# Raising TensorE's counts by a drain behind a group of matmuls, in a four-layer graph network

## The reference

```python
edge_index = jnp.stack([src, dst])
h = jnp.maximum(_layernorm(x, axis=-1), 0.0)
x = x + _L0_gnn_ref(h, edge_attr3_2x32, src, dst, ...)   # attention, softmax messages, summed by dst
...
x = x + _L1_gnn_ref(h, edge_index, 12500)                # segment_sum(h[src], dst)
...
x = x + _L2_gnn_ref(h, edge_index, edge_attr_4, edge_attr_8, 12500, ...)
# per edge: silu(silu(radial @ W1 + b1) @ W2 + b2) @ W3 + b3 gives 256 weights, multiplied with h[src] and summed by dst
...
x = x + _L3_gnn_ref(h, edge_index, ...)                  # 4-head attention, softmax over the edges of one src
```

## Time and profile before

| what | us |
|---|---|
| median of three runs without a profile | 9832.66 |
| lowest and highest of them | 9832.34, 9836.29 |
| span of the profiled execution | 12916.5 |
| busy in that span: TensorE matmuls | 5065.7 (39%) |
| weight loads | 2933.9 (23%) |
| VectorE | 6996.1 (54%) |
| ScalarE | 3814.9 (30%) |
| GpSimd | 7314.1 (57%) |

### The profile page before, as it was taken

One profiled execution on the slowest core, in us unless ns is written; L12 is line 12 of the kernel. 1 busy time (PEld: TensorE's weight loads), 2 busy tenths in 40 slices (PEclk: granted clock), 3 DMA queues, 4 the chain that ended last, 5 costly groups with the idle time before them and its releaser, 6 DMA issues. The chain is left out here.

```text
span 12916.5 us, 85174 instructions
## 1 busy us (share of the span) xinstructions
PE 5065.7 (39%) x24874; PEld 2933.9 (23%) x25115; DVE 6996.1 (54%) x11023; ACT 3814.9 (30%) x6015; POOL 7314.1 (57%) x7495
## 2 busy tenths in 40 slices
PE   2224300029135555555536777777613333300001
PEld 1214300002124444444422222222211111100001
DVE  5654488889452222222226777777614545457761
ACT  0002333336013333333312222222102333346640
POOL 5645577758554444444455556556563555566654
PEclk5556655569556666666667777777756666655555
DMA  6101366635300000000010111111010111133331
GB/s 237 45 20 39 112 219 212 213 128 184 110 20 15 17 17 17 17 15 17 16 31 21 24 22 23 23 23 25 21 19 1 44 32 31 35 93 126 122 101 39
DMA packets 466546, 815.90 MB, mean 63 GB/s; under 512 B 229189, under 2 KB 326902, under 8 KB 415526
## 3 DMA queue, kind: packets, MB, share of 16 engines
q10 hardware_dynamic: 81600, 447.60, 9.0%
q0 software_dynamic: 236352, 156.57, 6.9%
q1 hardware_dynamic: 148134, 206.27, 4.9%
HBM read 402.58 MB, written 407.23 MB: 63 GB/s over the span
## 5 line engine op out<-in xcount | busy, mean ns | idle before, releaser
L1609 POOL DMA_INDIRECT hs<-tab_h,src_i x3136 | 2975.3, 949 | 2771.9 <-issue 1164.6
L1201 POOL DMA_INDIRECT en<-tab_s,src_i x1568 | 1562.9, 997 | 863.9 <-issue 508.4
L1096 DVE SCALAR_TENSOR_TENSOR picked<-rank_ps,hot_hi 128x98 f32<-128x98 f32 x1568 | 313.1, 255 | 2131.9 <-remote 1139.7
L1888 PE MATMUL tp_ps<-w_pair,x 128*128 128x512 f32 x1568 | 1092.3, 786 | 569.8 <-DVE prod_b L2016 495.9
L2298 POOL DMA_INDIRECT rows_src<-out_rows,pos x784 | 750.7, 957 | 742.5 <-ACT out_rows L2344 468.0
L2420 DVE TENSOR_SCALAR hot_col<-count_up,pos_late 128x784 bf16<-128x784 f32 x560 | 564.9, 1029 | 747.2 <-remote 552.8
L2310 POOL DMA_INDIRECT hs<-tab_h,ptr x784 | 741.5, 946 | 378.2 <-issue 256.2
L2323 PE MATMUL late_ps<-hot_col,hot_row 128*128 128x512 bf16 x1075 | 517.8, 493 | 1010.0 <-DVE hot_col L2420 567.6
L997 PE MATMUL rank_ps<-place_sb,hot_t 128*128 128x98 f32 x3136 | 840.6, 385 | 0.0
L2013 DVE TENSOR_TENSOR prod_a<-tp_ps,zz 128x768 f32<-128x768 f32 x392 | 374.4, 955 | 721.4 <-remote 534.5
L1035 PE MATMUL turn_bank<-place_sb,ident 128*128 128x98 f32 x784 | 231.1, 389 | 1240.4 <-issue 634.9
(11 more groups left out here) (402 smaller groups left out, 16214.5 us busy)
## 6 DMA issues: line engine op xcount, KB each, us to landing
sums<-rows ACTq DMA_DIRECT2D x98, 1088.0 KB
sums<-rows ACTq DMA_DIRECT2D x147, 512.0 KB
ev_rows<-zeros ACTq DMA_DIRECT2D x16, 3136.0 KB
en_rows<-en SPq DMA_DIRECT2D x49, 1024.0 KB
raw<-ev_rows ACTq DMA_DIRECT2D x49, 1024.0 KB
en_back<-en_rows ACTq DMA_DIRECT2D x49, 1024.0 KB
r<-in_edge_attr_2x ACTq DMA_DIRECT2D x49, 1024.0 KB
y_rows<-r ACTq DMA_DIRECT2D x49, 1024.0 KB
```

Source lines behind the costliest of these rows:

```text
L1201: pool.indirect_dma_start(en[s][:, g, :], None, tab_s0, bass.IndirectOffsetOnAxis(ap=src_i[:, p * 2 * CH + g:p * 2 * CH + g + 1], axis=0)) ...
L1609: pool.indirect_dma_start(rows[k][:, g, :], None, tab_h, bass.IndirectOffsetOnAxis(ap=src_i[:, t * CH + g:t * CH + g + 1], axis=0)).then_i ...
L1888: nc.tensor.matmul(o, x2[k][:, a, b * EP:(b + 1) * EP], w3_cols, start=True, stop=False)
```

## The change

Where the increment of a semaphore hung on the last matmul or transpose of a group, that instruction now has none, and a drain is issued behind it on TensorE that carries the increment. This is done at ten places; the waits of the other engines and their values stay.

```diff
@@ def turn
                 for g in range(GR):
-                    last = nc.tensor.transpose(self.turn_ps[:, g, 0:EP], self.hot_lo[k][:, q * GR + g, :], identb[0:EP, 0:EP])
-                last.then_inc(self.turned, 1)
+                    nc.tensor.transpose(self.turn_ps[:, g, 0:EP], self.hot_lo[k][:, q * GR + g, :], identb[0:EP, 0:EP])
+                nc.tensor.drain().then_inc(self.turned, 1)
@@ def rank
-                last.then_inc(self.ranked, 1)
+                nc.tensor.drain().then_inc(self.ranked, 1)
@@ def group
-                last.then_inc(self.samed, 1)
+                nc.tensor.drain().then_inc(self.samed, 1)
...
-                last.then_inc(self.placed, 1)
+                nc.tensor.drain().then_inc(self.placed, 1)
@@ def count, in stages A and B
-                    last.then_inc(counted, 1)
+                    nc.tensor.drain().then_inc(counted, 1)
@@ def hidden1
-                    last.then_inc(hid, 1)
+                    nc.tensor.drain().then_inc(hid, 1)
@@ def hidden2
-                    nc.tensor.matmul(hid_ps[:, u % 3, 0:4 * EP], w2[:, :], x1[:, a, :], start=True, stop=True).then_inc(hid, 1)
+                    nc.tensor.matmul(hid_ps[:, u % 3, 0:4 * EP], w2[:, :], x1[:, a, :], start=True, stop=True)
+                    nc.tensor.drain().then_inc(hid, 1)
@@ def products
-                    last.then_inc(tpw, 1)
+                    nc.tensor.drain().then_inc(tpw, 1)
@@ def late
-                        last.then_inc(late_added, 1)
+                        nc.tensor.drain().then_inc(late_added, 1)
```

## The result

The changed kernel takes 10575.82 us (median of 4 runs, 10540.91 to 10601.76) against 9832.5 us of the kernel before, run beside it: a ratio of 1.0755, 95% interval 1.0742 to 1.0768. It is 743 us slower. The forecast was 9960, with a range up to 10210.

The account below looks back on a forecast made before the run. GpSimd's pace of indirect DMAs was taken to set nearly all of the four main stages. Drain costs of 92 + 20 + 10 + 5 = 127 us on 9833 gave 9960 us, range 9815 to 10210.

Parts of the forecast that it names:

- The budget: Four main stages: 6634 indirect DMAs at 1.25 us, 8292 us, plus 1535 us of other span make 9827 us.
- A, C and D: First-layer gathers and 14 ranked chunks; tensor weights; pointer columns, sends and last gathers: drains add 20, 10 and 5 us.
- in the profile alone: Whole trace: 3084 us of the 12916.5 us span taken as waiting that timed runs lack.
- The price of a stop: On TensorE's queue, a drain delays the next weight load by 0.34 us, or 0.41 at half clock.
- The sum at the upper level: Ranked chunk in the second-layer stage at full clock: 17.1 us plus 2.5 for drains, 19.6, under GpSimd's 20.0.
- From place step to transposes: Rank group on TensorE: sign expected in the changed trace, 2.6 us instead of 1.95.
- I take a quarter at half clock: Second-layer stage, 84 ranked chunks: a quarter at half clock gives 21.1 us a chunk after, 92 us in all.
- Half clock: Rival, chance 0.15: drains lower TensorE's activity so most chunks fall to 1.2 GHz; 462 us in second-layer stage, 10336 total.
- the half-clock chunk: Ranked chunk in the second-layer stage at half clock: 22.6 us without late counts, 25.5 with drains.
- "Turned" and "samed": Two rank-group drains: turned's push of the own and cross matmuls put at 0.07 us; samed's hidden behind ScalarE's copy.
- The late counts are real: Rival, chance 0.12: late matmul counts hold 265 us of the timed median; drains' counts may come in time, giving 9695.

Follow-up runs that it names:

- light_placed_ranked: Kernel before with 12 of 16 indirect DMAs left out in the second-layer gather stage and drains for placed and ranked alone: 11827.48 us, ratio 0.9164.
- light_filler4: Changed kernel with 12 of 16 second-layer indirect DMAs left out and four extra, overwritten 512-column matmuls in every rank group: 12578.46 us, ratio 0.9740.
- light_before_2: Kernel before, without drains, with 12 of 16 indirect DMAs left out in the second-layer gather stage: 11546.36 us, ratio 0.8972.
- ranks_only: Kernel before with drains for the four rank counts alone (turned, samed, placed, ranked; 1568 drains): 13652.29 us, ratio 1.0598.

## Why the prediction was wrong

**The budget was right, what it said of the profile wrong.** GpSimd's pace sets A, C and D in the quick condition, within 43 us each, as 1.25 us an operation said. But "in the profile alone" fell: whole timed comparisons run at the 12916 us of the trace of before. That trace was a run of another condition than its timed runs, and its waits and clocks were those of TensorE held up by late counts.

**The price of a stop was right in size.** 0.41 us at 1.2 GHz was forecast, 0.42 is measured. At 2.4 GHz 0.34 was forecast: in light_placed_ranked a group takes 4.39 us from place step to place step against 3.60, 0.39 for each of its two.

```profile
5001.17 0.43 PE L1035 MATMUL turn_bank<-place_sb,ident 128*128 128x98 f32 x2 [0.49 <-ACT hot_t L1054]
...
5005.56 0.43 PE L1035 MATMUL turn_bank<-place_sb,ident 128*128 128x98 f32 x2 [0.49 <-ACT hot_t L1054]
```

The sum at the upper level held too: 19.6 us a chunk with all drains was forecast, 19.95 is the chunk at clock 1.00 in the result's trace. From place step to transposes it is 2.75 us in light_filler4 (5010.46 to 5013.21), where 2.6 was forecast. The drains end some 0.02 us behind the modelled end of the last matmul (median in the changed kernel), where the earlier trace rows gave 0.05, and the Trainium skill's rule in "PSUM — Partial Sum Buffer", "Engine vs sequencer instructions", that a drain waits until the engine is idle, agrees: the load behind the drain starts 0.49 us after the last matmul's start, not with it.

**The step that failed: "I take a quarter at half clock".** In the changed kernel all ranked chunks but a few run at half clock. The share was taken as a property of the stage, the same before and after, when the change itself moves it: 0.83 without drains and 0.51 with them, with the lateness out of the way. For the kernel before the quarter was good: 18.5 us a chunk by it, 18.7 in light_before_2, where one group of four is slow. The rival "Half clock" had this mechanism and was given 0.15. The argument against it, that the trace of before had more stalls than a timed run, pointed the wrong way: its 0.66 came with stalls of 10 us between bursts at 1.00, and a stream with four short stops a group and no long ones has 0.51. What the clock stood at with few long waits said nothing about what it is with many short ones.

**And the half-clock chunk was too small.** 25.5 us was forecast "with drains at 0.41 and less hidden"; it is 29.05. The prediction let only 2.9 us of drains through, 25.5 - 22.6. (The 22.6 came from a chunk that the earlier trace rows show at full clock near its end; that it lies close to the 22.3 below is luck.) At 1.2 GHz TensorE's own stream is the loop (5.58 us a group without drains), so no stop is hidden beside another engine's work: all 16 count, 16 x 0.42 = 6.7. "Turned" and "samed", costed at 0.07 and 0, are as dear as the other two. By the prediction's own formula, all chunks at half clock and none hidden: (29.05 - 20.0) x 84 = 760, where it had 92, and 462 for the rival. Either half alone would have cost little. At 1.2 GHz without a drain a chunk would be at least 4 x 5.58 = 22.3 (an estimate; no run had it); with all drains and the clock left where it was, 18.8 + 4.0 = 22.8 (an estimate, the sum of the two pairs), and 19.95 with the clock at 1.00. Over GpSimd's 20.0 that is 2.3, 2.8 or nothing, at most some 240 us in 84 chunks. Together they make 760.

**A, C and D** were forecast at 20, 10 and 5 us. No more than 43, 35 and 35 can be there, what these stages stand over GpSimd's pace; how much is isn't shown. In the late condition the drains in C show, 223 us for 784 of them, 0.28 each where about 0.2 was put: C isn't at GpSimd's pace then.

**"The late counts are real" (0.12)** was nearly right in what it saw and wrong in what follows. The counts are late in timed runs, but only in the late condition, and a drain doesn't mend it: there the drains themselves end late. All records of the drain of `samed`, line 1029 (ns least, median, most; first and last start), first in ranks_only, then in the changed kernel of the result:

```profile
L1029 PEldq DRAIN  x392: 838/1570/10124, 1083.4 to 7289.4; - x196
```
```profile
L1029 PEldq DRAIN  x392: 927/1653/1655, 701.9 to 5534.6; - x196
```

## What to carry to other kernels

A drain in a stream of short matmul groups costs a stop, here 0.4 us, and the stops together can cost the clock, here 6 us of every 10: price both, and never carry the clock of the trace of before into the kernel after. Before a short stop is called hidden, do the sum at 1.2 GHz too, where TensorE may wait for nobody and so nothing hides. And if a trace's span doesn't match the timed runs, treat it as a trace of another condition: find a stage's floor from one engine's count and pace, and distrust its waits.

## What the runs showed of the hardware that was not expected

*More work made TensorE faster.* Two useless 512-column matmuls a group took a chunk from 29.05 to 24.5 us, clock 0.51 to 0.79. The Trainium skill's rule in "TensorE: Matmul & The Clock Gate", "Part 1: The HAM clock gate", that sustained activity lifts the throttle, has this direction.

*A stream busy for 2168 of 2691 us stayed at 1.2 GHz* for nearly the whole stage, and one busy for 1254 of 1837 had 0.83: the busy share of a row didn't tell the clock. (The same matmuls are busy for longer at 1.2 GHz.)

*Short stops kept the clock from coming back.* Without drains the clock came back within one group, 5.58 us, of an idle 3.71. With drains the same program ran a chunk in 19.95 us at 1.00 and then, behind an idle 2.11, at 0.50 for over 1100 us.

*Two conditions.* The kernel before took 9832 us in the first comparison and 12877 to 12920 in three others, on three chips. In the late condition TensorE's completions come late, whether a matmul or a drain carries them, and it goes with the indirect DMAs in flight: with 12 of 16 left out in B a chunk falls from 33.6 to 18.7 us without drains and from 41.8 to 29.05 with them, 14.9 and 12.7 us, and 29.05 is the value of the quick condition. In ranks_only ScalarE, idle for 8.76 us, starts the copy that waits for a drain 8.0 us after the last matmuls have run:

```profile
5030.76 0.84 PE L1028 MATMUL cross_ps<-hot_tb 128*128 128x384 bf16 x3
...
5039.62 0.60 ACT L1067 ACTIVATE own_same<-own_ps 128x512 bf16<-128x512 f32 x1 [8.76 <-PEq L1029]
```

Why those runs have it and the first comparison had none stays open. ranks_only has no run in the quick condition, so the split of the 743 us between the rank drains and the others is inferred, from the stages and chunks of the changed kernel's trace and from the 29.05.
